# A six-stage decoder kernel: attention's row maxima moved earlier, the last pairs of linear attention reordered, and the gated queries and gates computed as products of parts

## The reference, cut to what matters

```python
x = x + _L0_attn_ref(_layernorm(x), ...)
x = x + _L0_xattn_ref(_layernorm(x), ctx_2048, ...)   # softmax attention, 16 heads of 32, int8-rounded queries
x = x + _L0_ffn_ref(_layernorm(x), ...)               # shared expert and 16 routed experts
x = x + _L1_attn_ref(_layernorm(x), ...)              # linear attention, 32 heads of 64, decay, norm, gate
x = x + _L1_xattn_ref(_layernorm(x), ctx_2048, ...)   # gated linear cross attention
x = x + _L1_ffn_ref(_layernorm(x), ...)               # MXFP8-rounded feed-forward
```

```python
q = _feature_map(query @ Wq.T)                 # x + 1 for x > 0, else exp(x)
gate = jax.nn.sigmoid(query @ Wg.T + bg)
k, v = _feature_map(k), v                      # of kv @ Wkv.T
z = 1.0 / (einsum(q, k.sum) + EPS)
out = (einsum(q, k^T v) * z * gate) @ Wo.T
```

## Time and profile before

| | before |
|---|---|
| median of 3 runs | 2075.59 us (2070.09 to 2077.59) |
| the profiled execution, its own time | 2075.2 us |
| its span from the first to the last instruction | 2073.5 us |
| PE busy | 1904.0 us (92%) |
| DVE busy | 1229.0 us (59%) |
| ACT busy | 661.5 us (32%) |
| mean granted TensorE clock | 0.958 |

### The profile page before, as it was taken

The page is one execution under the profiler, slowest core; times in us unless marked ns, Lnnn a source line. Parts: engine busy times, 40 slices in busy tenths (PEclk is TensorE's granted clock), DMA queues, the critical chain, the costliest instruction groups (busy, mean ns, idle before and its releaser), DMA issues. The chain is left out here.

```text
span 2073.5 us, 25267 instructions
## 1 busy us (share of the span) xinstructions
PE 1904.0 (92%) x9749; PEld 1423.7 (69%) x9752; DVE 1229.0 (59%) x2148; ACT 661.5 (32%) x1053; POOL 225.9 (11%) x192
## 2 busy tenths in 40 slices
PE   7899796899998399998999999999989999899997
PEld 5677693344443258876888888888868745788886
DVE  5412646555551535548677777787774287866655
ACT  3311222344445125533333332342234231221211
POOL 0000001121110200001011101120120001122122
PEclk9999897799999689999999999999999999999999
DMA  5100402233220410013231331331212100111101
GB/s 204 41 0 1 153 21 54 61 70 69 57 59 1 123 41 1 1 33 107 71 100 36 130 105 30 106 110 69 83 67 82 62 21 21 43 39 42 41 1 41
DMA packets 67191, 124.15 MB, mean 60 GB/s; under 512 B 8576, under 2 KB 27008, under 8 KB 65536
## 3 DMA queue, kind: packets, MB, share of 16 engines
q1 hardware_dynamic: 67072, 122.53, 18.8%
HBM read 88.82 MB, written 14.68 MB: 50 GB/s over the span
## 5 line engine op out<-in xcount | busy, mean ns | idle before, releaser
L941 DVE TENSOR_REDUCE b_nm<-ps 128x1 f32<-128x1024 f32 x128 | 151.5, 1220 | 118.7 <-PE ps L862 118.5
L929 ACT ACTIVATE b_pr<-ps 128x512 f32<-128x512 f32 x256 | 132.3, 605 | 159.5 <-PE ps L880 159.5
L229 PE MATMUL ps<-d_x_high,d_w_high 128*128 128x512 f32 x384 | 154.2, 402 | 1.5 <-DVE d_x_low L1853 1.5
L231 PE MATMUL ps<-d_x_high,d_w_low 128*128 128x512 f32 x384 | 149.8, 390 | 0.0
L230 PE MATMUL ps<-d_x_low,d_w_high 128*128 128x512 f32 x384 | 149.7, 390 | 0.0
L892 PE MATMUL ps<-b_pr,b_VS 128*64 128x512 f32 x512 | 129.9, 631 | 0.0
L880 PE MATMUL ps<-b_qS,b_kS 98*128 98x512 f32 x256 | 93.0, 445 | 20.1 <-DMA b_qS<-b_nm_parts 17.7
L862 PE MATMUL ps<-b_kS,b_qS 96*128 96x512 f32 x256 | 94.9, 460 | 15.6 <-DMA b_qS<-b_q_parts 10.1
L880 PEld LDWEIGHTS ps<-b_qS,b_kS 98*128 98x128 f32 x256 | 44.1, 192 | 90.0 <-issue 50.6
L1727 POOL TENSOR_TENSOR d_sqsum<-d_sqsum,d_sq 128x512 f32<-128x512 f32 x32 | 44.7, 1398 | 473.0 <-ACT d_sq L1638 472.7
L229 PEld LDWEIGHTS ps<-d_x_high,d_w_high 128*128 128x128 f32 x384 | 72.2, 188 | 17.3 <-issue 2.1
(11 more groups left out here) (382 smaller groups left out, 4788.3 us busy)
## 6 DMA issues: line engine op xcount, KB each, us to landing
b_kS<-b_k_parts SPq DMA_DIRECT2D x96, 128.0 KB, 2.3
f_rows<-d_fw SPq DMA_DIRECT2D x24, 512.0 KB, 3.2
f_w<-f_rows SPq DMA_DIRECT2D x12, 1024.0 KB, 4.8
b_qS<-b_q_parts SPq DMA_DIRECT2D x96, 64.0 KB, 2.0
a_convT<-in_convT SPq DMA_DIRECT2D x4, 1024.0 KB, 13.3
b_ctxT<-in_ctxT SPq DMA_DIRECT2D x8, 512.0 KB, 5.2
d_w<-in_d_wq SPq DMA_DIRECT2D x16, 256.0 KB, 3.6
d_w<-in_d_wk SPq DMA_DIRECT2D x16, 256.0 KB, 2.8
```

The costliest lines, as they stand in the source:

```text
L229: nc.tensor.matmul(out, lhsT[0], rhs[0], start=start, stop=False)
L231: return nc.tensor.matmul(out, lhsT[1], rhs[0], start=False, stop=stop)
L929: nc.scalar.activation(pr[:, n % RING, :], c.ps[:, 4 + n % BANKS, :], ACT.Exp).then_inc(exp_done, 1)
L941: nc.vector.tensor_reduce(nm[:, g % 2, u:u + 1], c.ps[:, banks:banks + 2, :], AX.XY, ALU.max, negate=True).then_inc(job_read, 1)
```

## The change

Four edits.

1. Attention: the maxima run 6 slots ahead instead of 4, and the turn is at slot 11 instead of 13.
2. Linear attention, pair 0: its four projections run in the order queries of the first half of the tokens, keys of the first half, queries of the second, keys of the second (`part_of`).
3. Linear attention, last pairs: pair 15's first gate projection moves before pair 14's outputs, the second stays before pair 15's; one part of `round_weights` moves from pair 15 to pair 13; the low parts of pair 14's gated outputs come after pair 15's states; ACT makes the high part of the last output weights before the last gate; and of the four low parts of the context and its weights between the last adds, two move into the next stage's first block, where TensorE and SP wait for them.
4. Gated cross attention: `turn_normed` becomes `turn_and_split` (each of 8 tiles: ACT copies the high part, DVE subtracts for the low part). The two weights are split at the start of the next block, and queries and gates become `product_of_parts`. DVE keeps the eight shifts in the query loop but spreads the reciprocals: four in the query loop, four among the gate jobs.

```diff
-    LEAD, TURN_AT = 4, 13
+    LEAD, TURN_AT = 6, 11
...
+    def part_of(p, i):
+        return (i % 2, i // 2) if p == 0 else (i // 2, i % 2)
...
-                if j < 2:
+                if j < 4:
                     pe.wait_ge(x_low, 4 * (n + 1))
...
                 if p + 2 < PAIRS:
                     gates(p + 1)
-                elif p + 1 == PAIRS:
-                    gates(p)
+                elif p + 2 == PAIRS:
+                    gates(p + 1, (0,))
+                else:
+                    gates(p, (1,))
...
                 elif p + 1 < PAIRS:
-                    pair(p + 1, 0, 4)
+                    pair(p + 1, 0, 5)
                 else:
-                    pair(p, 4, 6)
                     high_outputs(SUMS - 1)
+                    pair(p, 5, 6)
...
-                    if between and t < len(c_splits):
+                    if between and t < 2:
...
-                if p >= 1:
+                if 1 <= p < PAIRS - 1:
                     for b in range(2):
                         low_gated(p - 1, b)
...
                 if 1 <= p < PAIRS - 1:
-                    round_weights(1)
+                    round_weights(2 if p == PAIRS - 3 else 1)
                 low_weights(p + 2, 0)
                 states(p)
                 if p == PAIRS - 1:
-                    round_weights(1)
+                    for b in range(2):
+                        low_gated(p - 1, b)
                     low_outputs(SUMS - 1)
...
+                if n == 3:
+                    sp.wait_ge(rest_low, 2)
...
+                    if j == 0 and bank == 4:
+                        pe.wait_ge(rest_low, 1)
+                    elif j == TILES:
+                        pe.wait_ge(rest_low, 2)
...
+            for _, _, raw, parts in c.context_rest:
+                nc.vector.tensor_tensor(parts[1], raw, parts[0].bitcast(F32), ALU.subtract).then_inc(rest_low, 1)
             dve.wait_ge(sum_done, 1)
...
-    turn_normed(c, "e")
+    turn_and_split(c, "e_t", *g.x_parts)
...
+    SPLITS = [(e.wqT, e.wq_parts), (e.wgT, e.wg_parts)]
+    INVERSES, LATE_INVERSES = {0: 0, 2: 1, 4: 2, 6: 3}, {1: 4, 2: 5, 4: 6, 5: 7}
...
+            for i, (raw, parts_) in enumerate(SPLITS):
+                dve.wait_ge(w_high, i + 1)
+                nc.vector.tensor_tensor(parts_[1][:], raw[:], parts_[0][:].bitcast(F32), ALU.subtract).then_inc(w_low, 1)
...
                 if j >= 1:
-                    inverse(j - 1)
-            inverse(NJ - 1)
+                    shift(j - 1)
+                    if j - 1 in INVERSES:
+                        inverse(INVERSES[j - 1])
+            shift(NJ - 1)
             for j, (b, m) in enumerate(JOBS):
+                if j in LATE_INVERSES:
+                    inverse(LATE_INVERSES[j])
...
+                pe.wait_ge(w_low, 1)
                 for k in range(KD):
-                    last = nc.tensor.matmul(c.ps[:, 4 + j % 2, :], e.wqT[:, k, m * P:(m + 1) * P],
-                                            c.xF[:, k, tokens(n)], start=k == 0, stop=k == KD - 1)
+                    last = product_of_parts(nc, c.ps[:, 4 + j % 2, :], [w_[:, k, m * P:(m + 1) * P] for w_ in e.wq_parts],
+                                            [x[:, k, tokens(n)] for x in e.x_parts], k == 0, k == KD - 1)
```

More of the change, by code:

```diff
@@ L1477, in queries_keys, with gates @@
                 for i in range(first, last):
-                    pe.wait_ge(w_low[i // 2], p + 1)
-                    project(first_job(p) + i, i // 2, i % 2)
-            def gates(p):
+                    part, n = part_of(p, i)
+                    pe.wait_ge(w_low[part], p + 1)
+                    project(first_job(p) + i, part, n)
+            def gates(p, halves=(0, 1)):
                 pe.wait_ge(w_low[2], p + 1)
-                for n in range(2):
+                for n in halves:
                     project(first_job(p) + 4 + n, 2, n)
@@ L1608, in pair @@
                     act.wait_ge(proj_done, j + i + 1)
-                    tok = slice(i % 2 * BANK, (i % 2 + 1) * BANK)
+                    part, n = part_of(p, i) if i < 4 else (2, i - 4)
+                    tok = slice(n * BANK, (n + 1) * BANK)
                     src = c.ps[:, (j + i) % 2, :]
@@ L1613, in pair @@
                         act.wait_ge(qd_done, 2 * p)
-                    if i == 2 and p >= 1:
+                    if part == 1 and p >= 1:
                         act.wait_ge(t_done, 2 * p)
@@ L1618, in pair @@
                     if i < 4:
-                        dst = (qF, kF)[i // 2][:, tok]
+                        dst = (qF, kF)[part][:, tok]
                         nc.scalar.activation(dst, src, ACT.Silu).then_inc(proj_moved, 1)
@@ L1622, in pair @@
                         nc.scalar.activation(ga[:, p % 2, tok], src, ACT.Sigmoid).then_inc(proj_moved, 1)
-                    if i % 2 == 1 and p + 1 < PAIRS:
-                        high_weights(p + 1, i // 2)
+                    if n == 1 and p + 1 < PAIRS:
+                        high_weights(p + 1, part)
             def values(g):
@@ L1715, in _ @@
                 for n in range(2):
-                    pool.wait_ge(proj_moved, first_job(p) + n + 1)
+                    pool.wait_ge(proj_moved, first_job(p) + (2 * n if p == 0 else n) + 1)
                     tok = slice(n * BANK, (n + 1) * BANK)
@@ L1906, in linear_attention @@
     c.rms = sqsum, ones, ms, y
+    c.context_rest = c_splits[2:]
 class GatedTensors:
@@ L1928, in __init__ @@
         self.bg = c.at("e_bg", [P, KD], F32, 50.5)
+        self.x_parts = [c.at("e_x_high", [P, KD, TOK], F32R, 16), c.at("e_x_low", [P, KD, TOK], F32R, 181)]
+        self.wq_parts = [c.at("e_wq_high", [P, KD, DM], F32R, 197), c.at("e_wq_low", [P, KD, DM], F32R, 52)]
+        self.wg_parts = [c.at("e_wg_high", [P, KD, DM], F32R, 32), c.at("e_wg_low", [P, KD, DM], F32R, 60)]
 def gated_cross_attention(c):
@@ L1944, in gated_cross_attention @@
     sum_done, ms_done, rs_done, x_done = (c.sem(f"e_{n}") for n in ("sum_done", "ms_done", "rs_done", "x_done"))
+    rest_low = c.sem("e_rest_low")
     k_done, k_exp, k_min, k_ready = (c.sem(f"e_{n}") for n in ("k_done", "k_exp", "k_min", "k_ready"))
@@ L2166, in mx_feed_forward @@
     e_out_done, e_added = c.sem("e_out_done"), c.sem("e_added")
+    w_high, w_low = c.sem("e_w_high"), c.sem("e_w_low")
+    SPLITS = [(e.wqT, e.wq_parts), (e.wgT, e.wg_parts)]
+    INVERSES, LATE_INVERSES = {0: 0, 2: 1, 4: 2, 6: 3}, {1: 4, 2: 5, 4: 6, 5: 7}
     JOBS = [(n, m) for n in range(2) for m in range(KD)]
@@ L2400, in _ @@
                     pe.wait_ge(gate_ready, j - 1)
+                pe.wait_ge(w_low, 2)
                 for k in range(KD):
-                    last = nc.tensor.matmul(c.ps[:, 6 + j % 2, :], e.wgT[:, k, m * P:(m + 1) * P],
-                                            c.xF[:, k, tokens(n)], start=k == 0, stop=k == KD - 1)
+                    last = product_of_parts(nc, c.ps[:, 6 + j % 2, :], [w_[:, k, m * P:(m + 1) * P] for w_ in e.wg_parts],
+                                            [x[:, k, tokens(n)] for x in e.x_parts], k == 0, k == KD - 1)
                 last.then_inc(gate_done, 1)
@@ L2467, in high @@
                 nc.scalar.activation(turn_parts(e)[0], turn_bank(e), ACT.Copy).then_inc(high_done, 1)
+            for raw, parts_ in SPLITS:
+                nc.scalar.activation(parts_[0][:], raw[:], ACT.Copy).then_inc(w_high, 1)
             for j in range(NJ):
```

3 lines of the change are left out of this document (2 added, 1 removed).

## The result

| | before | after |
|---|---|---|
| median | 2074.61 us (2070.09 to 2077.59, 4 runs) | 2043.26 us (2041.07 to 2045.01, 4 runs) |
| ratio to before | | 0.9858, 95% interval 0.9843 to 0.9874 |
| the profiled execution, its own time | 2075.2 us | 2045.01 us |
| its span | 2073.5 us | 2043.3 us |
| mean granted TensorE clock | 0.958 | 0.961 |

By the medians the change takes 31.3 us off, to 2043.26 where 2045 was forecast. The record's ratio is not the quotient of the two medians (that would be 0.9849); by it the gain is 29.5 us, and by its interval 26.1 to 32.6. The same kernel timed once more, beside the kernel before on one chip, gave 2043.94 and 2075.56, ratio 0.9853 (0.9837 to 0.9868).

A forecast was written before the change was run, and what follows sets the result against it. TensorE, busy 92% of the span, was taken as the bound. Terms -18.1 (attention), -3.0 (last pairs) and -9.7 (gated attention) gave -30.8 from 2075.2, forecast 2045 us; own range 2041 to 2050, whole range 2036 to 2059.

The forecast's parts named there:

- edit 1, attention: Attention's maxima: six boundaries -19.0, last boundary -1.4, pair-and-turn step +1.5, group 0's start +1.7, end -0.9: -18.1 us.
- edit 2, pair 0: Linear attention's pair 0: the 1.50 us stall moves behind the second projection; 0, between -0.2 and +0.2 us.
- edit 3, last pairs: End of linear attention: pair 14's outputs no longer wait, last sum's third tile 3.0 us earlier; -3.0, between 0 and -6.
- edit 4, move of x: Gated attention: DVE's eight low parts in a row end at 1638.3 instead of 1636.52: +1.8 us.
- edit 4, the summary's clock: Gated attention's summary after 3.3 us idle: lower clock only as a rival's second place, one stretch of 1.6 us; shared chance 0.17.
- edit 4, products: Gated query and gate jobs: 64 F32 products of 0.859 us become three F32R matmuls of 0.680: -11.5 us.
- Boundaries: Attention's group starts: wait of 1.57 us and 1.60 us of lower clock vanish, 3.17 each, six times: -19.0 us.
- 8.6 against 6.1 us: Attention: maxima's DMAs would begin 8.6 us before the group, against 6.1 us needed; 2.5 us left, so no wait.
- the clock in attention: Rival: attention's clock falls all the same once a group, keeping 1.6 of 3.17: 11 us more, 2056; chance 0.14.
- slot-10 stack: Rival: attention's wait moves to slot 10's stack (1.0 us room): 2065 to 2080, chance 0.03; grown, slower, 2088, chance 0.03.
- Start of attention: Group 0's slot 0 holds seven maxima instead of five at half clock: +1.7 us taken, bounds 1.2 and 3.4.
- a lower clock at new places: Rival: clock falls behind pair 15's masks and after the move of x, one stretch of 1.6 us each: 2048; chance 0.17.

The follow-up runs named there:

- lead-only: The changed kernel with the turn back at slot 13 and the lead of 6 kept (edits 2 to 4 stay): 2062.94 us, ratio to before 0.9954.
- turn-only: The changed kernel with the old lead of 4 and the turn kept at slot 11: 2040.69 us, ratio to before 0.9856.
- lead-4 kernel: The changed kernel with LEAD back at 4, turn at slot 11, nothing else altered: 2040.69 us, ratio to before 0.9856.
- reciprocals' kernel: The changed kernel with each reciprocal straight after its shift in the query loop, none in the gate jobs: 2048.67 us, ratio to before 0.9875.
- reordered kernel: The changed kernel with lead 4, last half gate projection before pair 15's second products, context's low parts after the last sum's first two adds: 2042.44 us, ratio 0.9859.

## Why the prediction was right, and where it was not

The time came out within 2 us, and in part by luck: its own terms add up to 25.5 us in the trace instead of 30.8, and 5.0 more came from a stage that it had no term for. The mechanisms that it named for the large terms, the wait for the rows with the clock behind it and the cheaper products, are the ones that the experiments show.

| term | predicted | in the trace |
|---|---|---|
| edit 1, attention | -18.1 | -16.7 |
| edit 2, pair 0 | 0 | 0 |
| edit 3, last pairs | -3.0 | -1.6 |
| edit 4, move of x | +1.8 | +2.0 |
| edit 4, the summary's clock | 0 (a rival) | +1.5 |
| edit 4, products | -11.5 | -10.7 |
| router and experts | 0 | -5.0 |

**Boundaries: right.** The waits and the stretch of lower clock behind each are gone, 3.17 us a group for groups 1 to 5. The lead-only and turn-only kernels show that it was the turn's place, as the arithmetic of 8.6 against 6.1 us had it: in the trace after the DMAs for group 2 begin at 444.85, 8.8 us before its first scores at 453.66. The step with pair and turn takes 5.72 us (445.76 - 440.04) against 4.97 + 0.64 = 5.61: 0.1 instead of the 0.24 forecast. Nothing waits for a stack, and the rivals of the clock in attention and of the slot-10 stack fell.

**Start of attention: mis-sized.** "I take 1.7, with 1.2 and 3.4 as bounds." Group 0 grew by 3.2 us though it lost a wait of 1.55, so the start cost 4.6 with the 0.1 above taken off, and the lead-4 kernel gives back those 4.6. The two further maxima cost about their 2.4 at DVE's pace (the first step takes 11.17 us instead of 8.63); what the bounds left out is that the clock stays down for 7 us more and the second step takes 7.16 instead of 5.05, where they had allowed one stretch of 1.6 on top of 1.8. In the reciprocals' kernel, where the clock rises earlier, the second step takes 5.39, and the start stays inside the bounds. The lead gives 2.1 back later, 0.9 forecast: above all the last step with a pair takes 4.10 us instead of the 5.81 of the lead-4 kernel, which has the last two maxima in that step beside the same pair and turn.

**Pair 0: right.** PE's timeline after shows the stall moved to the third projection:

```profile
933.04 0.63 PE L1449 MATMUL ps<-ident,xn 128*128 128x128 f32 x4 [1.50 <-DVE d_x_low L1861]
...
941.96 0.47 PE L229 MATMUL ps<-d_x_high,d_w_high 128*128 128x512 f32 x1 [1.70 <-issue]
```

It waits 1.70 where the second had waited 1.50, and starts 8.9 us after the turn of x as before (963.83 - 954.87 and 941.96 - 933.04). No run has edit 2 without edit 3; these rows are all that shows it.

**Last pairs: half, by a rival.** From the stage's row at 954.87 before and 933.04 after (the same turn of x), the last sum starts 1521.36 - 954.87 = 566.5 before and 1497.92 - 933.04 = 564.9 after: 1.6 less instead of 3.0. The masked products and updates are 0.9 and 0.6 us longer than before at clock 0.58, close to the price of 1.6 that the rival "a lower clock at new places" named, at the place that it named (idle of 2.1). All seven traces that have this wait of 2.1 us have the fall: in six the products take 1.91 to 2.08 us and the updates 2.18 to 2.45, in the one of edits 2 and 3 alone it comes with the updates (2.93). With DVE's old order, and with the gates in the gap, wait and fall are both gone. How much the lower clock behind the third tile takes differs: to the end of the last sum, linear attention is 1.5 us shorter in the first trace after and 2.9 in the second. That the third tile still waits 3.0 us and that the clock then falls was forecast; the reordered kernel shows that neither had to be: the context's low parts stood before two adds that TensorE waited for, with nobody waiting for them.

**Move of x: right; the summary's clock: the rival's second place.** Idle of 3.61 us after the transposes, and the clock falls in the summary, 1.5 us. It did so in 7 of the 10 traces that have edit 4 (15.7 to 15.9 us in six, 17.1 in that of edit 4 alone), and not in the other three (14.3 us), with the same idle time; with the 1.6 us of idle that the three traces without edit 4 have there, it fell in none. The Trainium skill ("TensorE: Matmul & The Clock Gate", Part 4: PE-mode transpose) says that transposes don't count as busy for the clock in the usual way; these traces agree in direction, since only transposes and idle time lie before the fall, but by that alone it would fall each time.

**Products: right, slightly too much.** The query jobs gave the 5.7 forecast. The gate jobs gave 5.0 instead of 5.8: 33.7 us against the 32.2 to 33 of the sum, without a wait for DVE, as 31.5 us of DVE's work fitted beside them. A gate job takes 4.06 us instead of 4.73 from start to start, 0.67 less where the sum had 0.72, and the first one only 0.34 less. Its twelve matmuls take 2.85 us behind the transposition, where the prediction took 2.72 from a run of nothing but such matmuls. The reciprocals' spread was taken as a condition of this, and it is: without it 4.3 of the 10.7 are lost. The Trainium skill ("TensorE: Matmul & The Clock Gate", Back-to-back issue gap) would have made the gain 13.6; the trace has 10.7, so the row was the better guide and still too generous.

**Router and experts: not in the prediction.** The lower clock lasts 49.5 us of this stretch in the trace of before, 49.4 with edits 2 and 3 alone, and 39 to 44 in all others; with edits 2 and 3 alone it is as long as before, 267.6 us, with edit 4 alone 262.5. Whether the long form is commoner in the unprofiled runs of the kernel before stays open: only one profiled execution of it exists. What the runs do say is that the profiled one was not a quick one: 46 other executions took 2068.1 to 2077.6 us, median 2072.0, and 9 of them 2075.2 or more; the long ones have the lower mean clocks (2077.3 us at 0.955, 2068.1 at 0.960). By the ratios, the parts timed by themselves are worth 17.4 and 19.9 (edit 1, twice), 1.0 and 7.9 us, 26 to 29 together; the whole is worth 29.5 and 30.5. With an uncertainty of about 3 us on each that is no contradiction, but it leaves room for a gain of a few us by such luck on either side.

## What to carry to other kernels

When a transfer is waited for at each turn of a loop, ask which one instruction releases it and move that one; moving the work before it as well only fills the loop's first slot, where everything piles up at the slower engine's pace and the slow clock. A wait filled on TensorE was worth its own length here and often 1.3 to 1.6 us more, but a wait opened elsewhere costs the same, so after a reorder list the idle stretches that are new, and fill them with work that is ready (here the last gate projection). And check the sum stage by stage against the trace even when the total fits: here 5 us that no term foresaw covered 5 that the terms fell short.

## What was not expected of the hardware

The same wait before the same instructions does not always bring the lower clock. In the lead-only kernel a wait of 1.56 us at 423.00 is followed by clock 1.00 and a step of 3.96 us, one of 1.59 at 458.93 by 0.69 and a step of 5.59. Group 0's second step took 7.16 us or 5.39. The summary after 3.6 us of idle fell to 0.71 or stayed at 1.00. And identical work in the router and experts took between 262.3 and 267.7 us in thirteen traces. The wait of 2.1 us at pair 15, by contrast, brought a fall each of seven times, only not always at the same instruction. The Trainium skill ("TensorE: Matmul & The Clock Gate", What's actually happening) says that the chip's watch over TensorE's activity runs freely and does not start with the kernel; these pairs agree with that, since equal work would then meet it at other moments, but no run here shows the watch itself. For an edit of this size it means that a price of the clock is a chance, and that one profile does not settle it.
